# Weighing values for four steps in a row instead of two, with a fifth buffer of exponentials

## The chip, the cores and the metric

The kernel runs on one core of a Trainium2 chip. The metric is the device time of one execution in microseconds (us), lower is better. Its engines: TensorE (PE, matrix products into the eight banks of PSUM), VectorE (DVE), ScalarE (ACT), GpSimd (POOL), and SyncE, which here only issues transfers. Each runs its own list of instructions in order; they meet at semaphores.

## What is computed

One transformer block on x of shape 4 x 2048 x 256: a modulated layer norm, causal attention with 16 heads of 16 columns and rotary position codes, a gated residual; then a second modulated layer norm and a soft mixture of eight experts, with another gated residual. The part that matters here:

```
q, k = rope(h @ Wq.T), rope(h @ Wk.T); v = h @ Wv.T     # 16 heads of 16
scores = einsum('bhqd,bhkd->bhqk', q, k) * scale
scores = where(causal, scores, lowest)
attn = softmax(scores, axis=-1)
out = einsum('bhqk,bhkd->bhqd', attn, v)
```

## The kernel before

The four batches run one after another. In each, attention is followed by the second norm and the experts, beside which the next batch's queries and keys are made. The change touches attention alone.

**Tiling.** Heads are taken four at a time (four groups), and for each group the 2048 queries in four chunks of 512. That makes 16 chunks, k = 0 to 15, with k = 4 * group + c. A **step** is one block of 128 keys against the chunk's 512 queries, for the four heads of the group. Chunk c has 4c full steps and then four on the causal diagonal, which use 512, 384, 256 and 128 queries. That is 4, 8, 12 or 16 steps for a chunk and 160 for a batch. A step is cut into **units**, each of which fills one PSUM bank: a full step has four (one for each head), the diagonal ones four, four, two and one. A batch has 560 units. Three banks (0 to 2) are for scores, used in turn.

**Three streams in PE's list.** (1) Score units: `score_unit` (line 717, with the causal mask added by line 721). It waits until ScalarE has taken the bank's last content. (2) Max units: the running maximum of each query has to be known before its scores are made, so a second set of score products (lines 631 to 642, 592 units a batch) goes to three other banks (3 to 5), and VectorE reduces each to maxima (line 1347, 640 reductions a batch). A max unit waits until VectorE has reduced the bank's last content. Max units run some chunks ahead of the score units; the table `MAXES_BY` fixes how many stand before each score unit, on the whole a little more than one for each. In the last chunk there are none. (3) Weighing: `weigh(s)` (line 737) multiplies the exponentials of step s with the values of its 128 keys, four float32 products, one for each head, side by side in four strips of 32 columns of the array, all added up in bank 6.

**ScalarE** takes each score unit out of PSUM through an exponential (line 1047) into a buffer of exponentials in SBUF: `Eb`, four buffers, step s in buffer s % 4 (`ESLOTS = 4`). At the first unit of a step it waits until the step that had the buffer before is weighed. At the end of a chunk it copies bank 6 out (line 1041).

**VectorE**, beside the reductions, runs at the end of each chunk of maxima a chain of five small operations (lines 1364 to 1373) and a copy (line 1343), and once a chunk it divides the output by the sum (lines 1434 and 1436).

**The order** is written out by hand. After each score unit u, PE runs what `WEIGH_AFTER` has for u: steps are weighed in pairs. Steps s and s + 1 (s even) come three units (`WEIGH_BEHIND`) after the last unit of s + 1. Since every chunk's number of steps is a multiple of four, pairs never cross chunks. In the last chunk, the projection and the second norm of the earlier chunks run beside the scores (`beside`), and the squares of that norm go to the 8 KB behind the other buffers (`squares`, at 14336 of R2).

Of the kernel before, what the change touches and what calls it, by code (L numbers as in the profile page):

```python
# [9 lines left out]
P = 128  # L10
NT = T // P
NC = 4
CH = T // NC
# [12 lines left out]
NST = 3  # L26
# [7 lines left out]
HG = 4  # L34
NG = H // HG
NK = NG * NC
VC = HD + 1


def steps_of_chunk(k):  # L40

    return 4 * (k % NC) + 4


STEPS = [(k, j) for k in range(NK) for j in range(steps_of_chunk(k))]
NSTEP = len(STEPS)
# [4 lines left out]
def diagonal(s):  # L51

    k, j = STEPS[s]
    return max(j - 4 * (k % NC), -1)
# [8 lines left out]
SU = len(UNITS)  # L63
FIRST_UNIT = [[u[0] for u in UNITS].index(s) for s in range(NSTEP)]
LAST_UNIT = [FIRST_UNIT[s + 1] - 1 if s + 1 < NSTEP else SU - 1 for s in range(NSTEP)]
# [75 lines left out]
WEIGH_BEHIND, EVAC_BEHIND, TURN_BEHIND, GATHER_BEHIND = 3, 5, 8, 9  # L141


def after_units(last, behind):

    out = {}
    for i, u in enumerate(last):
        out.setdefault(u + behind, []).append(i)
    return out
# [1 line left out]

LAST_UNIT_OF_CHUNK = [LAST_UNIT[LAST_STEP[k]] for k in range(NK)]

WEIGH_AFTER = after_units([LAST_UNIT[s | 1] for s in range(NSTEP)], WEIGH_BEHIND)
EVAC_AFTER = after_units(LAST_UNIT_OF_CHUNK, EVAC_BEHIND)
TURN_AFTER = after_units(LAST_UNIT_OF_CHUNK, TURN_BEHIND)
GATHER_AFTER = after_units(LAST_UNIT_OF_CHUNK, GATHER_BEHIND)

SLOTS_AFTER = after_units(LAST_UNIT_OF_CHUNK[NC:2 * NC], GATHER_BEHIND + 3)
ESLOTS = 4  # L160

QU = 2 * NC
HIDDEN_BANK = [6, 0]
# [20 lines left out]
def set_of(b, i):  # L184
    return i % SETS_OF_BATCH[b]


def set_parked(b, i):

    before = [(d, j) for d in range(b + 1) for j in range(QU) if d < b or j <= i]  # L190
    return 32 * sum(set_of(d, j) == set_of(b, i) for d, j in before)
# [3 lines left out]
def adaln_block(nc, x, Wq, Wk, Wv, Wo, norm_gamma, slot_gamma, slot_embeds, w1, b1, w2, b2, cond, wmod,  # L195
# [12 lines left out]
    with ctx:  # L208
        def sb(name, shape, dt=f32):
            return ctx.enter_context(nc.sbuf_tensor(name, shape, dt))  # L210

        def sem(name):
            return ctx.enter_context(nc.semaphore(name))
# [41 lines left out]
        R2 = sb("R2", [P, 16384])  # L255
# [3 lines left out]
        def view(r, a, n, dt=f32):  # L259
            v = r[:, a:a + n]  # L260
            return v if dt == f32 else v.bitcast(dt)
# [1 line left out]

        kst = [view(R1, 8192 * i, 4096, bf16).rearrange("p (h t) -> p h t", h=HG) for i in range(2)]
        qst = [view(R1, 8192 * i + 4096, 4096, bf16).rearrange("p (h t) -> p h t", h=HG) for i in range(2)]
        Eb = [view(R2, 2048 * i, 2048).rearrange("p (h t) -> p h t", h=HG) for i in range(ESLOTS)]
        vall = view(R2, 8192, NT * H * VC).rearrange("p (t h c) -> p t h c", t=NT, h=H)
        outT = [view(R2, 12800 + 512 * i, 512) for i in range(2)]
        otok = view(R4, 0, 4096).rearrange("p (t d) -> p t d", d=D)
# [49 lines left out]
        ps = ctx.enter_context(nc.psum_tensor("ps", [P, 8, 512], f32))  # L319
# [40 lines left out]
        s_pk = [sem(f"parts_parked{i}") for i in range(RSETS)]  # L360
# [11 lines left out]
        s_pvq = sem("step_weighted")  # L372
# [183 lines left out]
        def _(pe):  # L556
            mm, tr = nc.tensor.matmul, nc.tensor.transpose
# [3 lines left out]
            for w in range(2):  # L561
                for k in range(KD):
                    for r in range(2):
                        last = tr(ps[:, w, (2 * k + r) * P:(2 * k + r + 1) * P], pw[:, w, r, k * P:(k + 1) * P], ident[:, :])
            last.then_inc(s_pt, 1)
            pe.wait_ge(s_silu, 1)
            for k in range(KD):
                last = tr(ps[:, 4, k * B:k * B + B], pc[0:B, k * P:(k + 1) * P], ident[0:B, 0:B])
# [3 lines left out]
            for i, q in enumerate((0, 1, 6, 7, 2, 3, 8, 9)):  # L572
                for f in range(KD):
                    last = mm(ps[:, 4, P + i * B:P + i * B + B], wmod_sb[:, f, q * P:(q + 1) * P], siluT[:, f, :],
                              start=f == 0, stop=f == 1)
# [115 lines left out]
            for n, bank in ((0, 6), (1, 0)):  # L691
                for f in range(KD):
                    last = mm(ps[0:B, bank, :], siluT[:, f, :], wmod_sb[:, f, (n + 1) * 512:(n + 2) * 512],
                              start=f == 0, stop=f == 1)
# [9 lines left out]
            for b in range(B):  # L704

                def score_unit(u):

                    s, h0, n, w = UNITS[u]
                    k, j = STEPS[s]
                    g, c = divmod(k, NC)  # L710
                    if s == FIRST_STEP[k] and u == FIRST_UNIT[s]:
                        pe.wait_ge(s_bias[k % 3], (b * BIAS_USES[k % 3] + k // 3 + 1) * 64)
                    if u >= NST:
                        pe.wait_ge(s_ex, b * SU + (u + 1 - NST))
                    bank = ps[:, u % NST, :]
                    for i in range(n):
                        last = mm(bank[:, i * w:(i + 1) * w], kst[g % 2][0:BROWS, h0 + i, j * P:(j + 1) * P],  # L717
                                  qst[g % 2][0:BROWS, h0 + i, (c + 1) * CH - w:(c + 1) * CH],
                                  start=i == 0, stop=True, skip_group_check=True)
                    if diagonal(s) >= 0:  # L720
                        last = mm(bank[:, 0:n * w].rearrange("p (n w) -> p n w", n=n)[:, :, 0:P], identb[:, :],  # L721
                                  maskTb[:, 0:n, :], start=False, stop=True, skip_group_check=True)
                    last.then_inc(s_st, 1)

                def weigh(s):

                    k, j = STEPS[s]
                    g, c = divmod(k, NC)
                    w = CH - max(diagonal(s), 0) * P
                    if j == 0:  # L730
                        if k:
                            pe.wait_ge(s_ev, b * NK + k)
                        else:
                            pe.wait_ge(s_vone, b + 1)
                    pe.wait_ge(s_ex, b * SU + (LAST_UNIT[s] + 1))
                    for h in range(HG):
                        last = mm(ps[32 * h:32 * h + VC, 6, CH - w:CH], vall[:, j, HG * g + h, :], Eb[s % ESLOTS][:, h, 0:w],  # L737
                                  start=j == 0, stop=True, skip_group_check=True)
                    last.then_inc(s_pvq, 1)

# [73 lines left out]
                for u in range(SU):  # L814
# [3 lines left out]
                    score_unit(u)  # L818
                    for s in WEIGH_AFTER.get(u, ()):
                        weigh(s)  # L820
# [5 lines left out]
                    if u in BESIDE_AT:  # L826
                        beside(BESIDE_AT.index(u))
                for s in range(NSTEP):
                    if LAST_UNIT[s | 1] + WEIGH_BEHIND >= SU:
                        weigh(s)  # L830

                def logits(n):
# [64 lines left out]
                for n in range(NT):  # L897
# [3 lines left out]
                    for i in range(4):  # L901

                        k, mh = (i % 2, i // 2) if n == NT - 1 else (i // 2, i % 2)
                        last = mm(ps[:, 2 * k + mh, :], xn[:, n, k * P:(k + 1) * P], L[:, n, mh * 512:(mh + 1) * 512],  # L904
                                  start=n == 0, stop=n == NT - 1)
# [63 lines left out]
        def _(act):  # L969
            A = nc.scalar.activation  # L970
# [8 lines left out]
            for w in range(2):  # L979
                for k in range(KD):  # L980
                    last = nc.scalar.copy(wqkT[:, k, 2 * w:2 * w + 2, :].rearrange("p r t -> p (r t)"),
                                          ps[:, w, k * 256:(k + 1) * 256])
# [43 lines left out]
            for e in range(E):  # L1026
                last = A(psquares[:, e, :], pse[:, e, :], ACT.Square, accum_out=ssq[:, e:e + 1])
            last.then_inc(s_pss, 1)

            for b in range(B):  # L1030
# [10 lines left out]
                    nc.scalar.copy(outT[k % 2], ps[:, 6, :]).then_inc(s_ev, 1)  # L1041

                for u, (s, h0, n, w) in enumerate(UNITS):
                    if u == FIRST_UNIT[s] and s >= ESLOTS:
                        act.wait_ge(s_pvq, b * NSTEP + (s + 1 - ESLOTS))
                    act.wait_ge(s_st, b * SU + (u + 1))
                    A(Eb[s % ESLOTS][:, h0:h0 + n, 0:w], ps[:, u % NST, 0:n * w].rearrange("p (n w) -> p n w", n=n),  # L1047
                      ACT.Exp, scale=SCALE).then_inc(s_ex, 1)
                    if u == LAST_UNIT_OF_CHUNK[1]:
                        act.wait_ge(s_out, b * 16 * NC) if b else None  # L1050
                        for i in range(QU - SETS_OF_BATCH[b], QU):
                            act.wait_ge(s_pk[set_of(b, i)], set_parked(b, i))
                        act.wait_ge(s_mpark, 16)
                        load_group(act, 1, slice(0, T), s_ld[1])
                    for g in range(2, NG):
                        if u == LAST_UNIT_OF_CHUNK[NC * (g - 1) - 1]:
                            load_group(act, g, slice(0, T), s_ld[g % 2])
                    for k in EVAC_AFTER.get(u, ()):
                        evacuate(k)
                    if b == 0:  # L1060
                        for j in SLOTS_AFTER.get(u - 2, ()):
                            act.wait_ge(s_pt, 4 + j)
                            k, half = divmod(j, 2)
                            A(snT[:, k, half * 512:(half + 1) * 512], ps[:, 7, :], ACT.Identity, scale=gamcol[:, k:k + 1]
                              ).then_inc(s_pe_, 1)
# [75 lines left out]
                for e in range(E):  # L1141
# [3 lines left out]
                    for j in range(JH):  # L1145
                        last = A(hTe[e % 2][:, j, :], ps[:, HIDDEN_BANK[e % 2] + j // 4, (j % 4) * P:(j % 4 + 1) * P], ACT.Gelu,  # L1146
                                 bias=b1T[:, e * JH + j:e * JH + j + 1])
# [528 lines left out]
```

## Time and profile before

| | us |
|---|---|
| median of 3 runs | 3226.12 |
| lowest and highest | 3223.44, 3234.1 |
| the profiled execution | 3226.97 |
| its span in the trace | 3225.1 |

| engine | busy us | share of the span |
|---|---|---|
| PE | 3028.2 | 94% |
| VectorE | 2249.3 | 70% |
| ScalarE | 1754.8 | 54% |
| GpSimd | 340.8 | 11% |

The page gives busy time over the whole span, which mixes stages with different limits. A busy PE is not one that works at its rate: each matmul is shown with its whole way through the array, about 0.38 us for one of 512 columns, though the next one starts 0.22 us behind it. So what limits a stage is read from the distances between starts, and from the idle time in brackets at the end of a row of the timeline, with the engine and the line that ended it. A row of the timeline merges like instructions that follow each other ("x8"). In rows of line 737, "x16" is a pair of steps: eight products, each recorded as two.

### The profile page before, as it was taken

Reading aid. Unit: us, or ns where it says so; the run is one execution under the profiler, and the core shown is the slowest. Engines: PE = TensorE matmul, PEld = TensorE weight load, DVE = VectorE, ACT = ScalarE, POOL = GpSimd, SP = SyncE. Lnnn points to the kernel's source line nnn. Section 1 sums busy time; section 2 is a strip of 40 time slices with the busy share of each in tenths; the row PEclk is TensorE's granted clock in tenths of the full one; section 3 lists DMA queues with packets and bytes.
Section 4 is the critical chain, followed back from the end, with each engine's and each line's share of the span. In section 5 each row is a group of like instructions: output and inputs, shape, how many; then the busy total and the mean of one; then the engine's idle time right before and its main releaser. Section 6 shows DMA issues by size and latency. Waiting matters only on the chain.

```text
span 3225.1 us, 45179 instructions
## 1 busy us (share of the span) xinstructions
PE 3028.2 (94%) x17474; PEld 1535.5 (48%) x17651; DVE 2249.3 (70%) x4388; ACT 1754.8 (54%) x3189; POOL 340.8 (11%) x196
## 2 busy tenths in 40 slices
PE   6699999989999999998999999999999999999899
PEld 4233334447653333454774333345477333334468
DVE  5888887572778878756388888866448888885722
ACT  3356666564236666645515666664541666665550
POOL 4100000320400000112040000011222000002200
PEclk9899999999999999999999999999999999999999
DMA  5222201015412220002542202000453221100052
GB/s 153 79 41 41 41 1 40 15 57 205 150 35 34 41 41 27 21 7 92 196 138 54 41 1 41 28 21 7 145 178 116 41 41 26 17 27 27 33 180 75
DMA packets 124260, 206.12 MB, mean 64 GB/s; under 512 B 10223, under 2 KB 107189, under 8 KB 120425
## 3 DMA queue, kind: packets, MB, share of 16 engines
q1 hardware_dynamic: 110460, 153.07, 14.5%
q10 hardware_dynamic: 13584, 50.15, 8.4%
q8 instruction: 140, 2.29, 0.3%
q14 instruction: 76, 0.61, 0.1%
HBM read 160.21 MB, written 42.19 MB: 63 GB/s over the span
## 4 chain that ended last, share of the span: by engine, by line
PE 76%; DVE 15%; ACT 5%; issue 2%; ACTq 1%; DMA 1%; POOL 0%; SPq 0%; DVEq 0%
PE ps L737 14%; DVE pm L1347 12%; PE ps L717 9%; PE ps L642 9%; PE ps L904 7%; PE ps L843 7%; PE ps L655 7%; PE ps L935 4%; PE ps L602 3%; PE ps L924 3%; ACT R L1047 2%; PE ps L783 2%; PE ps L676 2%; PE ps L634 2%; PE ps L856 2%
## 5 line engine op out<-in xcount | busy, mean ns | idle before, releaser
L1347 DVE TENSOR_REDUCE pm<-ps 128x1 f32<-128x512 f32 (+4 forms) x2560 | 1380.5, 603 | 292.1 <-PE ps L642 193.5
L1047 ACT ACTIVATE R<-ps 128x512 f32<-128x512 f32 (+1 forms) x2240 | 1177.3, 592 | 652.0 <-PE ps L717 425.0
L717 PE MATMUL ps<-R 99*128 99x512 bf16 (+3 forms) x2560 | 829.8, 350 | 17.6 <-ACT R L1047 7.8
L642 PE MATMUL ps<-R 96*128 96x512 bf16 x1536 | 580.9, 386 | 39.4 <-DVE pm L1347 34.6
L737 PE MATMUL ps<-R 128*17 128x512 f32 (+3 forms) x5120 | 531.6, 533 | 4.9
L642 PEld LDWEIGHTS ps<-R 96*128 96x128 bf16 x1536 | 147.7, 97 | 437.3 <-DVE pm L1347 363.0
L717 PEld LDWEIGHTS ps<-R 99*128 99x128 bf16 x2560 | 241.9, 98 | 155.1 <-ACT R L1047 67.1
L655 PE MATMUL ps<-R 128*128 128x257 f32 x1024 | 247.2, 382 | 7.2 <-ACT R L991 3.6
L737 PEld LDWEIGHTS ps<-R 128*17 128x17 f32 x5120 | 118.2, 97 | 281.9 <-issue 168.4
L904 PE MATMUL ps<-R 128*128 128x512 f32 x512 | 230.0, 611 | 18.0 <-ACT R L1119 18.0
L843 PE MATMUL ps<-snT,R 128*128 128x512 f32 x512 | 230.1, 593 | 0.0
L1221 POOL TENSOR_TENSOR rstd<-veps,neghalf 128x4 f32<-128x4 f32 x16 | 16.2, 1013 | 1859.2 <-DVE veps L1457 1858.8
L655 PEld LDWEIGHTS ps<-R 128*128 128x128 f32 x1024 | 188.9, 190 | 48.4 <-issue 12.8
L904 PEld LDWEIGHTS ps<-R 128*128 128x128 f32 x512 | 99.7, 196 | 150.4 <-issue 140.8
L721 PE MATMUL ps<-maskTb,identb 128*128 128x128 bf16 (+2 forms) x671 | 159.8, 238 | 0.0
L1073 ACT ACTIVATE R<-ps,rnorm 128x1024 f32<-128x1024 f32 x64 | 71.4, 1116 | 147.9 <-PE ps L843 147.9
L1594 DVE TENSOR_TENSOR R<-ps,R 128x256 f32<-128x256 f32 x32 | 13.6, 425 | 187.7 <-PE ps L935 187.7
L843 PEld LDWEIGHTS ps<-snT,R 128*128 128x128 f32 x512 | 92.9, 190 | 94.8 <-issue 94.6
L935 PE MATMUL ps<-R 128*128 128x256 f32 x512 | 123.0, 396 | 9.2 <-ACT R L1146 7.7
L634 PE MATMUL ps<-R 96*128 96x128 bf16 x1024 | 100.6, 220 | 32.2 <-DVE maskTb L1397 13.5
L924 PE MATMUL ps<-R 128*128 128x128 f32 x1024 | 119.3, 275 | 8.5 <-DVE R L1585 8.5
L924 PEld LDWEIGHTS ps<-R 128*128 128x128 f32 x1024 | 118.4, 192 | 13.0 <-DVE R L1585 11.8
(159 smaller groups left out, 3142.8 us busy)
## 6 DMA issues: line engine op xcount, KB each, us to landing
R<-in_L_ffn_w_dram SPq DMA_DIRECT2D x64, 1024.0 KB, 6.1
R<-q_parts ACTq DMA_DIRECT2D x12, 768.0 KB
R<-k_parts ACTq DMA_DIRECT2D x12, 768.0 KB
q_parts<-R SPq DMA_DIRECT2D x16, 512.0 KB, 3.6
k_parts<-R SPq DMA_DIRECT2D x16, 512.0 KB, 3.5
R<-in_L_attn_x_dram SPq DMA_DIRECT2D x4, 2048.0 KB, 8.7
x_park<-R SPq DMA_DIRECT2D x16, 512.0 KB, 2.6
R<-x_park SPq DMA_DIRECT2D x16, 512.0 KB, 5.5
```

What stands on the lines that cost most here:

```text
L634: last = mm(ps[:, bank, i * P:(i + 1) * P], qt(4 * c + i), kt(4 * c + i, 1), start=False, stop=True, skip_group_check=True)
L642: last = mm(ps[:, bank, :], qt(4 * c + r), kt(4 * kc, 4), start=True, stop=True)
L655: last = mm(ps[:, 6 + n % 2, 0:D + 1], EcT[:, e, n * P:(n + 1) * P], eo[:, e, :], start=e == 0, stop=e == E - 1)
L717: last = mm(bank[:, i * w:(i + 1) * w], kst[g % 2][0:BROWS, h0 + i, j * P:(j + 1) * P], qst[g % 2][0:BROWS, h0 + i, (c + 1) * CH - w:(c + ...
L721: last = mm(bank[:, 0:n * w].rearrange("p (n w) -> p n w", n=n)[:, :, 0:P], identb[:, :], maskTb[:, 0:n, :], start=False, stop=True, skip_ ...
L737: last = mm(ps[32 * h:32 * h + VC, 6, CH - w:CH], vall[:, j, HG * g + h, :], Eb[s % ESLOTS][:, h, 0:w], start=j == 0, stop=True, skip_grou ...
L843: last = mm(ps[:, 4 - 2 * (n % 2) + mh, :], xnT[:, k, n * P:(n + 1) * P], snT[:, k, mh * 512:(mh + 1) * 512], start=k == 0, stop=k == 1)
L904: last = mm(ps[:, 2 * k + mh, :], xn[:, n, k * P:(k + 1) * P], L[:, n, mh * 512:(mh + 1) * 512], start=n == 0, stop=n == NT - 1)
L924: last = mm(ps[:, HIDDEN_BANK[e % 2] + j // 4, (j % 4) * P:(j % 4 + 1) * P], w1s[e % NR][:, k, j * P:(j + 1) * P], slotsT[:, k, e * P:(e + ...
L935: last = mm(ps[:, 4 + e % 2, 0:D], hTe[e % 2][:, j, :], w2s[e % NR][:, j, :], start=j == 0, stop=j == JH - 1)
L1047: A(Eb[s % ESLOTS][:, h0:h0 + n, 0:w], ps[:, u % NST, 0:n * w].rearrange("p (n w) -> p n w", n=n), ACT.Exp, scale=SCALE).then_inc(s_ex, 1)
L1347: mx = lambda o, i: V.tensor_reduce(o, i, AX.X, ALU.max)
```

## The change

Weighing is put in groups of four: `weighed_with(s)` gives the step behind whose last unit s is weighed. It is the last of its four steps (s | 3) everywhere but for the full steps of the last chunk, which stay in pairs (s | 1). PE therefore weighs 43 times a batch and not 80.

Four steps stay in their buffers longer, so there are five, the fifth over the place of `squares`. `place_exponentials` gives each step its buffer, its place in it and the step whose weighing frees it. The last diagonal step (128 queries) shares the buffer of the second one, behind its 384 columns. In the last chunk only the first four buffers are handed out. ScalarE waits for the weighing of the step that had the buffer, and at the first use of the fifth in the first batch for a transfer out of the same place.

```diff
+def weighed_with(s):
+
+    return s | 3 if diagonal(s) >= 0 or STEPS[s][0] < NK - 1 else s | 1
+
+
+WEIGH_AFTER = after_units([LAST_UNIT[weighed_with(s)] for s in range(NSTEP)], WEIGH_BEHIND)
-WEIGH_AFTER = after_units([LAST_UNIT[s | 1] for s in range(NSTEP)], WEIGH_BEHIND)
...
-ESLOTS = 4
+
+ESLOTS = 5
+
+
+def place_exponentials():
+
+
+    places, last = [], {}
+    for s in range(NSTEP):
+        if diagonal(s) == 3:
+            places.append((places[s - 2][0], CH - P, None))
+            last[places[s][0]] = s
+            continue
+        slot = min(range(ESLOTS - (STEPS[s][0] == NK - 1)), key=lambda x: last.get(x, x - ESLOTS))
+        places.append((slot, 0, last.get(slot)))
+        last[slot] = s
+    return places
...
-        Eb = [view(R2, 2048 * i, 2048).rearrange("p (h t) -> p h t", h=HG) for i in range(ESLOTS)]
+        Eb = [view(R2, 2048 * i if i < 4 else 14336, 2048).rearrange("p (h t) -> p h t", h=HG) for i in range(ESLOTS)]
...
-                        last = mm(ps[32 * h:32 * h + VC, 6, CH - w:CH], vall[:, j, HG * g + h, :], Eb[s % ESLOTS][:, h, 0:w],
+                        last = mm(ps[32 * h:32 * h + VC, 6, CH - w:CH], vall[:, j, HG * g + h, :], Eb[slot][:, h, at:at + w],
...
-                    if u == FIRST_UNIT[s] and s >= ESLOTS:
-                        act.wait_ge(s_pvq, b * NSTEP + (s + 1 - ESLOTS))
+                    slot, at, freed_by = EPLACES[s]
+                    if u == FIRST_UNIT[s] and freed_by is not None:
+                        act.wait_ge(s_pvq, b * NSTEP + (freed_by + 1))
+                    elif u == FIRST_UNIT[s] and slot == 4 and b == 0:
+
+                        act.wait_ge(s_pk[3], set_parked(0, 3))
```

What this moves in PE's list, at four full steps of chunk 2 in the first batch. Before, with line 737 the weighing (x8 is a pair), 717 a score unit, 642 and 631 to 640 max units; the two pairs stand eight score units apart, and of the rows between them the last ones are shown:

```order
367 L737 MATMUL ps<-R 17x512 x8
368 L642 MATMUL ps<-R 128x512
369 L717 MATMUL ps<-R 128x512
370 L642 MATMUL ps<-R 128x512
...
383 L717 MATMUL ps<-R 128x512
384 L642 MATMUL ps<-R 128x512
385 L717 MATMUL ps<-R 128x512
386 L737 MATMUL ps<-R 17x512 x8
```

Now (line 763 is the weighing, 742 a score unit, 656 to 667 max units), all four stand where the second pair stood:

```order
360 L665 MATMUL ps<-R 128x256
361 L667 MATMUL ps<-R 128x512
362 L742 MATMUL ps<-R 128x512
363 L763 MATMUL ps<-R 17x512 x16
364 L667 MATMUL ps<-R 128x512
365 L742 MATMUL ps<-R 128x512
```

Nothing else has moved against the score units: the max units stand where they did.

On the diagonal, after chunk 2 in the same batch, the first pair stood right behind the chunk's last score unit, and the second three units later:

```order
470 L717 MATMUL ps<-R 128x128 x4
471 L721 MATMUL ps<-maskTb,identb 128x512
472 L737 MATMUL ps<-R 17x512 x4
473 L737 MATMUL ps<-R 17x384 x4
474 L642 MATMUL ps<-R 128x512
475 L717 MATMUL ps<-R 128x512
```

Now the four are together, behind the third unit of the next chunk:

```order
474 L742 MATMUL ps<-R 128x512
475 L746 MATMUL ps<-maskTb,identb 128x128
476 L763 MATMUL ps<-R 17x512 x4
477 L763 MATMUL ps<-R 17x384 x4
478 L763 MATMUL ps<-R 17x256 x4
479 L763 MATMUL ps<-R 17x128 x4
480 L662 MATMUL ps<-R 128x128
```

The products are the same in number and size.

## Rows read from the trace of the kernel before

**Rows 1.** Busy us of PE, PEld, DVE, ACT, POOL, and PE's clock, in a stretch.
```profile
940.00:1312.00 372.00, 357.15 (x2500) 137.40 (x2540) 306.85 (x640) 247.04 (x472) 0.00 (x0) 1.00 0.18 33
```

**Rows 2.** Timeline of PE, steady part: start, length, instructions, [idle before <- what ended it].
```profile
1099.76 0.38 PE L717 MATMUL ps<-R 99*128 99x512 bf16 x1
1100.07 1.91 PE L737 MATMUL ps<-R 128*17 128x512 f32 x16
1101.91 0.39 PE L642 MATMUL ps<-R 96*128 96x512 bf16 x1
1102.14 0.38 PE L717 MATMUL ps<-R 99*128 99x512 bf16 x1
```

**Rows 3.** Timeline of PE's weight loads inside the pair of rows 2.
```profile
1100.51 0.12 PEld L737 LDWEIGHTS ps<-R 128*17 128x17 f32 x4 [0.31 <-issue]
1100.94 0.12 PEld L737 LDWEIGHTS ps<-R 128*17 128x17 f32 x4 [0.31 <-issue]
```

**Rows 4.** Timeline of PE, between two pairs where eight max units meet eight score units.
```profile
1315.46 0.39 PE L642 MATMUL ps<-R 96*128 96x512 bf16 x1
...
1316.06 0.39 PE L642 MATMUL ps<-R 96*128 96x512 bf16 x1
...
1317.79 1.91 PE L737 MATMUL ps<-R 128*17 128x512 f32 x16
```

**Rows 5.** Timeline of VectorE behind the pair of rows 4.
```profile
1320.06 4.74 DVE L1347 TENSOR_REDUCE pm<-ps 128x1 f32<-128x512 f32 x9 [1.07 <-PE ps L642]
```

**Rows 6.** Timeline of VectorE, full steps of chunks 5 to 7, second batch.
```profile
1067.22 6.69 DVE L1347 TENSOR_REDUCE pm<-ps 128x1 f32<-128x512 f32 x12
1075.14 4.88 DVE L1347 TENSOR_REDUCE pm<-ps 128x1 f32<-128x512 f32 x8 [1.23 <-PE ps L642]
...
1089.82 4.88 DVE L1347 TENSOR_REDUCE pm<-ps 128x1 f32<-128x512 f32 x8 [0.45 <-PE ps L642]
1096.00 5.27 DVE L1347 TENSOR_REDUCE pm<-ps 128x1 f32<-128x128 f32 x10 [1.30 <-PE ps L638]
1102.34 3.08 DVE L1347 TENSOR_REDUCE pm<-ps 128x1 f32<-128x512 f32 x5 [1.07 <-PE ps L642]
...
1123.67 5.11 DVE L1347 TENSOR_REDUCE pm<-ps 128x1 f32<-128x256 f32 x10 [0.80 <-PE ps L640]
1130.05 4.67 DVE L1347 TENSOR_REDUCE pm<-ps 128x1 f32<-128x512 f32 x9 [1.27 <-PE ps L642]
1136.07 1.29 DVE L1347 TENSOR_REDUCE pm<-ps 128x1 f32<-128x512 f32 x2 [1.34 <-PE ps L642]
...
1142.94 5.27 DVE L1347 TENSOR_REDUCE pm<-ps 128x1 f32<-128x512 f32 x10 [1.60 <-PE ps L642]
1149.38 4.88 DVE L1347 TENSOR_REDUCE pm<-ps 128x1 f32<-128x512 f32 x8 [1.17 <-PE ps L642]
1155.61 5.27 DVE L1347 TENSOR_REDUCE pm<-ps 128x4 f32<-128x512 f32 x10 [1.36 <-PE ps L634]
```

**Rows 7.** Timeline of VectorE, diagonals of chunks 4, 5 and 6.
```profile
1059.46 1.29 DVE L1347 TENSOR_REDUCE pm<-ps 128x1 f32<-128x512 f32 x2 [0.98 <-PE ps L642]
...
1081.10 1.89 DVE L1347 TENSOR_REDUCE pm<-ps 128x1 f32<-128x512 f32 x3 [1.08 <-PE ps L642]
1083.29 3.67 DVE L1347 TENSOR_REDUCE pm<-ps 128x1 f32<-128x512 f32 x7 [0.30 <-PE ps L642]
...
1114.60 1.09 DVE L1347 TENSOR_REDUCE pm<-ps 128x1 f32<-128x128 f32 x3 [1.70 <-PE ps L638]
1115.72 0.19 DVE L1364 TENSOR_REDUCE negm<-pm 128x16 f32<-128x32 f32 x1
```

**Rows 8.** Timeline of ScalarE beside rows 4.
```profile
1314.34 4.16 ACT L1047 ACTIVATE R<-ps 128x512 f32<-128x512 f32 x8 [1.73 <-PE ps L717]
```

**Rows 9.** Timeline of PE, the pairs on the diagonal of chunk 6.
```profile
1112.54 1.70 PE L737 MATMUL ps<-R 128*17 128x512 f32 x16
...
1115.96 0.84 PE L737 MATMUL ps<-R 128*17 128x256 f32 x16
```

## What the change does to the time: the prediction

> **What bounds the kernel now.** I first read the busy time of a stretch, to see whether one engine fills the stage that the change touches; then the timeline of PE, for the distances between starts; then VectorE's, for when it is idle and what ends that.
>
> In 372 us of the second batch's attention VectorE is busy 306.85 us, ScalarE 247.04 [rows 1]. PE's 357.15 is inflated, since each matmul is shown with its way through the array. From starts: a score or max unit of 512 columns costs PE 0.22 us, and a pair of weighed steps 1.84 us (1100.07 to 1101.91) [rows 2]. Four full steps are 16 score units, about 17 max units and two pairs: 33 x 0.22 + 2 x (1.84 + 0.09) = 11.1 us, the 0.09 being the lag in front of a pair (1099.76 to 1100.07 is 0.31, not 0.22) [rows 2]. They take longer: two pairs lie between the idle times at 1136.07 and 1149.38, 13.31 us apart, and between 1089.82 and 1102.34, 12.52 us [rows 6]. So PE is not at its limit. Rows 4 show why: in that stretch max units start 0.60 us apart (1315.46, 1316.06), not 0.44, and 0.61 is what a VectorE reduction takes (4.88 us for 8) [rows 4, 6]. The three max banks are full, PE waits for VectorE, and since PE's list is in order the scores behind wait too.
>
> VectorE is idle nearly only when PE weighs: it empties its three banks and then waits for the first max unit behind the pair. The idle times in rows 5 to 7 are these. **So the time of this stage is VectorE's work plus its idle time behind the pairs.** The work is untouched. Everything turns on whether the idle time grows or shrinks.
>
> **The switches.** A pair's weight loads come 0.43 us apart [rows 3], so its products need 4 x 0.43 = 1.72 us; it costs 0.09 + 1.84, so 0.21 us is entering and leaving. 37 pairs less in each of four batches, 148, save PE 148 x 0.21 = 31 us. Where PE waits 0.16 us at each max unit (0.60 against 0.44), this only lengthens the wait and is worth nothing. The Trainium skill, TensorEngine Tiling (Array Packing), Key Properties, says that changing the tiling mode drains TensorE; the 0.12 us that a pair takes over its 1.72 are such a price. By that rule alone the time would fall, by the 31 us worked out before.
>
> **Full steps, the main term.** A merged group puts 1.72 us more of weighing into one place. What VectorE can do meanwhile does not grow: it has at most three full banks. At one pair it was saturated: the pair at 1317.79 left it idle for 1.07 us, until 1320.06 [rows 4, 5]. From the pair's end (1317.79 + 1.84 = 1319.63) to VectorE's start are 0.43 us. So 1.84 + 0.43 - 1.07 = 1.20 us is the work it had in store when the pair began. Two saturated pairs leave 2 x 1.07 = 2.14 us idle, one group of four 1.07 + 1.72 = 2.79. The store is used once instead of twice.
>
> Not every pair is saturated, so I take one group of heads, chunks 4 to 7, which has six sets of four full steps. Idle behind the first pair of each, which goes: 0 (the 6.69 us of reductions from 1067.22 run through, since a division and the gate's product were in VectorE's list there), 0.45, 1.07, 0.80, 1.34, 1.17 [rows 6]: 4.83 us. Added behind the second pairs: 6 x 1.72 = 10.32. But five of the second pairs now show 1.23, 1.30, 1.27, 1.60 and 1.36 [rows 6], more than the saturated 1.07, as PE came to them with less in VectorE's banks; with sixteen score units since the last weighing instead of eight the banks will be full, which gives back 6.76 - 5 x 1.07 = 1.41. Net 10.32 - 4.83 - 1.41 = 4.08 us for six, 0.68 each. There are 21 sets a batch; at the last of them the max units end, which leaves 20 x 4 = 80: **+54 us**. Without the giving back a set costs 0.915, +73. If all first pairs were like the saturated one (1.07), with no other work in their shadow, it would be 1.72 - 1.07 - 1.41 / 6 = 0.42, +33.
>
> **Diagonals.** The first pair lasts 1.63 us, the second 0.77 (the rows' 1.70 and 0.84, less the 0.07 by which rows 2's 1.91 exceeds 1.84) [rows 2, 9]; together 2.40. Saturated, they would leave 2.40 + 0.43 - 1.20 = 1.63 idle, against 1.08 + 0.30 at chunk 5 [rows 7]: +0.25, and I take chunk 7 to be like it. At chunk 6 the chain of five small operations starts at 1115.72, just before the second pair, and behind it are the full banks, so VectorE has some 2.0 us in hand by my estimate (0.8 of chain, 1.2 of store); idle becomes 0.83 against 1.70: -0.87 [rows 7, 9]. Chunk 4, like 6 but with 0.98 before [rows 7], gives -0.15. Sum -0.52 for four; 56 diagonals with max units around them are 14 fours: **-7 us**. It lies between +14 (all like chunk 5) and -20.
>
> **The rest.** ScalarE needs 0.52 us for a unit (4.16 for 8) and waits 1.73 us behind a pair [rows 8]. With four steps it waits some 3.5, and 16 x 0.52 = 8.3 us fit into the 9.6 that remain of 13.1. Its waits for buffers: a set's second step takes the buffer of the first step of the set before; that one is weighed first in a group which stands before the second step's scores in PE's list, so the wait ends first. The fifth buffer's wait in the first batch is for a transfer made before attention begins: nothing. The last set of chunk 14 and its diagonal come when the maxima are done; two switches less are -2 us for four batches, a delay of 1.84 us for each batch would be +7; I take 0, as neither engine is full there. The last chunk keeps its pairs, and its diagonal steps come at the end in either order.
>
> **Sum.** 54 - 7 = +47 us. On the profiled execution (3226.97 us, of which 3225.1 are its span) that is 3274; it stands 0.85 us over the median, so 3273 for a median.
>
> **Rivals.** (1) *PE is the bound after all.* If VectorE's store were larger than I read, the longer weighing would be covered, PE's waits for it would go, and the 31 us of switches would come back: 3195. For it: PE's high busy time in rows 1, and in rows 2 a pair that starts right behind its score unit. Against: the 0.60 us steps of rows 4. A set now has 4.83 + 6.76 us over six of them, 1.9 us, of idle; to stay under that, a group of four would need 0.9 us more in store than the 1.20 seen. (2) *Balance.* A set costs the 0.42 of the lower bound, diagonals give back 20 and the end 2: 33 - 20 - 2 = +11, or somewhat less: 3227 to 3237. For it: unsaturated pairs such as the 1.60. (3) *More.* No giving back, diagonals at +14, the end at +7: +94, 3320. For it: first pairs with 0 and 0.45, whose weighing was nearly free.
>
> The Trainium skill, TensorEngine Tiling (Array Packing), PSUM Bottleneck, warns that packing speeds up TensorE but not the emptying of PSUM; the trace agrees, since max units wait for reductions of 0.61 us each. It changes nothing in the sum and speaks for the forecast against rival 1.
>
> **How the numbers follow.** The store of three banks explains all idle times of VectorE read here, so the forecast with its spread (3237 to 3320) has 0.74; balance 0.12, PE as the bound 0.13, beyond 3320 0.01. A measurement of this kernel can tell about 0.3% (10 us) from no change, so balance is nearly all of "same". Faster 0.13, same 0.12, slower 0.75. The range 3226 to 3310 leaves out the faster case and the highest end.
>
> **What would show it.** In the profile after: a group of four lasting 3.56 us; VectorE idle 2.6 to 2.9 us behind most of them at full steps, and 0.8 to 1.6 on diagonals; max units 0.60 us apart over most of a set, not only at its end; a set of four full steps 0.7 us longer; no idle of ScalarE that a weighing ended. I am wrong if the idle behind a group stays near 1.9 us, or if VectorE's reductions themselves become shorter.

## The result: 2.1% slower

| | median us | lowest to highest | runs |
|---|---|---|---|
| before | 3227.57 | 3223.44 to 3234.1 | 4 |
| changed | 3296.41 | 3292.98 to 3298.38 | 4 |

The ratio is 1.021, with a 95% interval of 1.019 to 1.0231: 69 us more. Forecast were 47 more (3273 for the median, 3226 to 3310 the range). The span of the profiled execution went from 3225.1 to 3291.1 us.

Two rows of the page carry the reading. They are the reductions of the maxima and the exponentials, with busy time, mean length, and the idle time of their engine just before them:

```profile
L1377 DVE TENSOR_REDUCE pm<-ps 128x1 f32<-128x512 f32 (+4 forms) x2560 | 1370.8, 600 | 362.8 <-PE ps L667 201.7
L1077 ACT ACTIVATE R<-ps 128x512 f32<-128x512 f32 (+1 forms) x2240 | 1189.9, 594 | 706.0 <-PE ps L742 395.3
```

Before, the page had these two as:

```profile
L1347 DVE TENSOR_REDUCE pm<-ps 128x1 f32<-128x512 f32 (+4 forms) x2560 | 1380.5, 603 | 292.1 <-PE ps L642 193.5
L1047 ACT ACTIVATE R<-ps 128x512 f32<-128x512 f32 (+1 forms) x2240 | 1177.3, 592 | 652.0 <-PE ps L717 425.0
```

VectorE does the same 2560 reductions, and is idle 70.7 us longer in front of them; its busy time is 9.7 us less. The sum of both has grown by 61 of the 66 us. So the time is where the prediction looked for it. (Why busy time shrinks: reductions that follow each other overlap a little. The rows show 0.67 to 0.69 us for one alone and 4.88 for eight, 0.61 each. Fewer interruptions, more overlap.)

One thing beside it differs. TensorE's granted clock has two levels, 2.4 and 1.2 GHz, and its mean, as a share of the full clock, is 0.980 in this profile and 0.986 in the one before: about 130 us at the lower level against 90. Much of the difference lies in the first chunks of the first batch (from 130 to 195 us the mean is 0.84, before 0.97). What this is worth is taken up with the sum below.

The timeline of PE, at the second set of chunk 7 in the second batch. A group of four stands there, and behind it max units (line 667) and score units (line 742) in turn:

```profile
1171.06 0.38 PE L742 MATMUL ps<-R 99*128 99x512 bf16 x1
1171.36 3.63 PE L763 MATMUL ps<-R 128*17 128x512 f32 x32
1174.92 0.39 PE L667 MATMUL ps<-R 96*128 96x512 bf16 x1
...
1176.10 0.39 PE L667 MATMUL ps<-R 96*128 96x512 bf16 x1
1176.33 0.38 PE L742 MATMUL ps<-R 99*128 99x512 bf16 x1
1176.70 0.39 PE L667 MATMUL ps<-R 96*128 96x512 bf16 x1
1176.92 0.38 PE L742 MATMUL ps<-R 99*128 99x512 bf16 x1
1177.29 0.39 PE L667 MATMUL ps<-R 96*128 96x512 bf16 x1
```

From 1171.36 to 1174.92 are 3.56 us, twice 1.72 and 0.12: one switch is saved. From 1176.10 on the max units start 0.60 and 0.59 us apart, as in rows 4: PE waits for VectorE again. VectorE's timeline around it:

```profile
1162.18 5.87 DVE L1377 TENSOR_REDUCE pm<-ps 128x1 f32<-128x512 f32 x11 [2.99 <-PE ps L667]
...
1171.23 0.21 DVE L1373 COPY nrow<-ps 48x128 bf16<-48x128 bf16 x1
1171.36 0.67 DVE L1377 TENSOR_REDUCE pm<-ps 128x1 f32<-128x512 f32 x1
1175.35 10.05 DVE L1377 TENSOR_REDUCE pm<-ps 128x1 f32<-128x512 f32 x18 [3.31 <-PE ps L667]
1188.47 1.68 DVE L1377 TENSOR_REDUCE pm<-ps 128x4 f32<-128x512 f32 x4 [3.07 <-PE ps L659]
```

Idle 2.99, 3.31 and 3.07, and between them no pause of VectorE of 0.15 us or more. At the same three places rows 6 have 1.27, 1.60 and 1.36. Each has grown by 1.71 or 1.72 us, the two steps' weighing that was put there. The first pairs' 0.80, 1.34 and 1.17 are gone. The other three sets of rows 6, in chunks 5 and 6, do the same:

```profile
1104.75 6.67 DVE L1377 TENSOR_REDUCE pm<-ps 128x1 f32<-128x512 f32 x11 [2.94 <-PE ps L667]
...
1126.81 8.26 DVE L1377 TENSOR_REDUCE pm<-ps 128x1 f32<-128x128 f32 x15 [3.02 <-PE ps L663]
...
1139.92 0.69 DVE L1377 TENSOR_REDUCE pm<-ps 128x4 f32<-128x512 f32 x1 [2.15 <-PE ps L659]
```

The first two were 1.23 and 1.30, and the third was 0.43, in a row of before that rows 6 leave out:

```profile
1108.56 0.69 DVE L1347 TENSOR_REDUCE pm<-ps 128x4 f32<-128x512 f32 x1 [0.43 <-PE ps L634]
```

The diagonals of chunks 5 and 6:

```profile
1112.92 3.67 DVE L1377 TENSOR_REDUCE pm<-ps 128x1 f32<-128x512 f32 x7 [1.51 <-PE ps L667]
...
1148.96 1.13 DVE L1377 TENSOR_REDUCE pm<-ps 128x1 f32<-128x256 f32 x2 [0.85 <-PE ps L665]
```

Forecast were 1.63 and 0.83, from 1.38 and 1.70 [rows 7]. The other two that the forecast used came out otherwise: at chunk 4 it is 0.32 where 0.83 was worked out, and at chunk 7 the diagonal's idle time went from 2.91 to 2.31, where +0.25 was taken.

To compare kernels, I add up VectorE's idle times in the timeline (those shown, from about 0.15 us up) between the start of a set's first weighing and the start of the next set's, over the 80 sets of full steps and the 56 diagonals with max units around them:

| | idle per set of full steps | idle per diagonal | sum against before | span against before |
|---|---|---|---|---|
| before | 2.03 | 1.53 | | |
| changed | 3.05 | 1.35 | +82 - 10 = +72 | +66.0 |

### The profile page after: what moved, and what is told of

It reads as the page before. It is cut to its first block, busy times and chain, and to the rows that moved or that the text cites. A ratio compares the mean times of both kernels' runs of the same rounds, so it can differ in the third digit from the quotient of the medians.

```text
span 3291.1 us, 45128 instructions
## 1 busy us (share of the span) xinstructions
PE 3067.5 (93%) x17489; PEld 1540.4 (47%) x17651; DVE 2250.1 (68%) x4388; ACT 1766.9 (54%) x3189; POOL 340.2 (10%) x196
## 3 DMA queue, kind: packets, MB, share of 16 engines
q1 hardware_dynamic: 110460, 153.07, 14.3%
## 4 chain that ended last, share of the span: by engine, by line
PE 73%; DVE 18%; ACT 5%; issue 2%; DMA 1%; SPq 1%; ACTq 0%; POOL 0%; DVEq 0%
PE ps L763 15%; DVE pm L1377 15%; PE ps L667 8%; PE ps L742 8%; PE ps L930 7%; PE ps L869 7%; PE ps L680 7%; PE ps L961 4%; PE ps L627 3%; PE ps L950 3%; ACT R L1077 2%; PE ps L809 2%; PE ps L701 2%; PE ps L882 1%; PE ps L659 1%
## 5 line engine op out<-in xcount | busy, mean ns | idle before, releaser
L1377 DVE TENSOR_REDUCE pm<-ps 128x1 f32<-128x512 f32 (+4 forms) x2560 | 1370.8, 600 | 362.8 <-PE ps L667 201.7
L1077 ACT ACTIVATE R<-ps 128x512 f32<-128x512 f32 (+1 forms) x2240 | 1189.9, 594 | 706.0 <-PE ps L742 395.3
L667 PE MATMUL ps<-R 96*128 96x512 bf16 x1536 | 588.4, 391 | 69.0 <-DVE pm L1377 59.9
L763 PE MATMUL ps<-R 128*17 128x512 f32 (+3 forms) x5120 | 506.6, 535 | 0.6
L763 PEld LDWEIGHTS ps<-R 128*17 128x17 f32 x5120 | 133.3, 98 | 313.4 <-issue 249.8
```

The lines of the kernel that those rows point to most:

```text
L667: last = mm(ps[:, bank, :], qt(4 * c + r), kt(4 * kc, 4), start=True, stop=True)
L1077: A(Eb[slot][:, h0:h0 + n, at:at + w], ps[:, u % NST, 0:n * w].rearrange("p (n w) -> p n w", n=n), ACT.Exp, scale=SCALE).then_inc(s_ex, 1)
L1377: mx = lambda o, i: V.tensor_reduce(o, i, AX.X, ALU.max)
```

## The experiments

All are variants of the changed kernel, so their line numbers are those of the profile after. Ratios are against runs of the kernel before on the same chip.

| run | median us | ratio | 95% interval |
|---|---|---|---|
| e1_pairs_five_buffers | 3224.36 | 0.9996 | 0.9986 to 1.0006 |
| e2_four_at_full_steps | 3290.41 | 1.0200 | 1.0185 to 1.0215 |
| e3_four_at_diagonals | 3221.85 | 0.9986 | 0.9976 to 0.9995 |
| e4_one_at_a_time | 3245.43 | 1.0060 | 1.0045 to 1.0075 |
| e5_short_maxima_pairs | 3122.28 | 0.9682 | 0.9669 to 0.9695 |
| e6_short_maxima_fours | 3125.20 | 0.9691 | 0.9678 to 0.9704 |
| e7_short_maxima_ones | 3200.03 | 0.9920 | 0.9906 to 0.9933 |
| e8_ones_in_last_chunk | 3217.36 | 0.9973 | 0.9964 to 0.9983 |
| e9_maxima_between_fours | 3257.34 | 1.0094 | 1.0080 to 1.0107 |
| e10_fours_at_diagonals_ones_last | 3211.52 | 0.9955 | 0.9942 to 0.9967 |
| e11_changed_again | 3295.66 | 1.0207 | 1.0190 to 1.0223 |
| e12_four_at_full_again | 3289.49 | 1.0198 | 1.0182 to 1.0214 |

### The buffers alone

```diff
 def weighed_with(s):
-    return s | 3 if diagonal(s) >= 0 or STEPS[s][0] < NK - 1 else s | 1
+    return s | 1
```

> The changed kernel, but every step is weighed with its pair as before; the five buffers, their places and their waits stay. Theory (the loss is VectorE's idle time behind longer weighings): 3227 us, nothing within 10 us of the kernel before. Rival (the loss comes from the fifth buffer: its place, or ScalarE's new waits): 3296 us or most of the way to it.

It is the kernel before within 0.1%. With pairs, the fifth buffer, its place and its waits cost nothing, and all of the loss comes from weighing in fours.

### Fours at full steps, and at diagonals

```diff
-    return s | 3 if diagonal(s) >= 0 or STEPS[s][0] < NK - 1 else s | 1
+    return s | 3 if diagonal(s) < 0 and STEPS[s][0] < NK - 1 else s | 1
```

> Four in a row at full steps only, the diagonal steps in pairs as before. Theory: the traces put +82 us on the 80 sets of full steps and -10 us on the diagonals, so without the diagonals' merging this is slower than the changed kernel: about 3306 us (3300 to 3315). Rival (long weighings cost the same wherever they stand, 148 merges sharing 69 us): 84 of 148 merges, 3227 + 39 = 3266 us.

```diff
-    return s | 3 if diagonal(s) >= 0 or STEPS[s][0] < NK - 1 else s | 1
+    return s | 3 if diagonal(s) >= 0 else s | 1
```

> Four in a row at diagonal steps only, full steps in pairs. Theory: VectorE's idle time falls by about 10 us there, 3217 us (3210 to 3225). Rival (every merge costs alike): 64 of 148 merges, 3227 + 30 = 3257 us.

The full steps alone give the whole loss; 64 of the 148 merges, those on the diagonals, are no loss and between pairs a gain of 4 us. A price for each merge, the same wherever it stands, falls: it asked for 3266 and 3257. My own number for the full steps was wrong too, by 16 us: I had added VectorE's 82 us of idle time without what is given back elsewhere. In the trace of e2 the idle time per set is 3.00 and per diagonal 1.58, +80 us, and the span grew by 66.8. The page's row for the reductions:

```profile
L1377 DVE TENSOR_REDUCE pm<-ps 128x1 f32<-128x512 f32 (+4 forms) x2560 | 1370.8, 601 | 366.9 <-PE ps L667 230.1
```

Busy and idle together are 65.1 us more than before, 74.8 of idle time less 9.7 given back by overlap of the reductions. That is nearly the whole 66.8.

The table's sets leave out the end of chunk 14 and the last chunk. There the merged diagonals do something that the forecast had at nothing. From the first score unit of the last chunk to its last, PE's timeline has 43.4 us in every batch before, in e1 and in e2, and 44.9 in every batch of e3 and of the changed kernel: 6 us for four batches. ScalarE's row behind that weighing, in the second batch, before and after:

```profile
1346.98 1.08 ACT L1047 ACTIVATE R<-ps 128x512 f32<-128x512 f32 x2 [2.32 <-PE ps L717]
```

```profile
1383.11 1.08 ACT L1077 ACTIVATE R<-ps 128x512 f32<-128x512 f32 x2 [3.82 <-PE ps L742]
```

The four diagonal steps of chunk 14 now stand together, three units into the last chunk, and ScalarE waits for the scores behind them: 1.50 us more. Against this stands the end of chunk 14. From the first score unit of its full set to the last chunk there are 25.2 us before, 23.4 in e3, 26.9 in e2 and 25.1 in the changed kernel.

> The changed kernel once more, beside e12 on the same chip. The theory has merged diagonals as a small gain in it: this should be 4 to 10 us under e12_four_at_full_again. The first two measurements had it 6 us over (3296 against 3290), on different chips.

> Fours at full steps, pairs at the diagonals, as e2_four_at_full_steps. Theory: 4 to 10 us over e11_changed_again. If it is equal or under it, what the merged diagonals give back between pairs is lost again between fours.

They came out at 3295.66 (3286.55 to 3299.72) and 3289.49 (3286.14 to 3298.11). The runs overlap, so nothing can be said on which is faster; that merged diagonals gain 4 us or more beside merged full steps, as I expected, is not confirmed. Idle per diagonal is 1.34 against 1.58 in the two traces, -13 us, but per full set it is 3.09 against 2.90, +15. Set by set, these 15 have two sources. Nine sets during which the granted clock fell to 1.2 GHz in one trace or the other, eight of them in e11, hold 8.9 us. The other 6.1 are a matter of counting: they lie in the set just before the diagonal of a chunk with eight full steps, and since the merged diagonal is weighed later, that set's stretch ends later and takes in idle time that e12 has in the diagonal's. All other sets agree within 0.05 us. So the diagonals give back about 7 us here and not 13, and the last chunk takes 6 of them.

### One step at a time

```diff
-    return s | 3 if diagonal(s) >= 0 or STEPS[s][0] < NK - 1 else s | 1
+    return s if STEPS[s][0] < NK - 1 else s | 1
```

> The other way: each step weighed by itself, three units behind its last unit, but for the last chunk, which keeps pairs. Theory: a full step's weighing is 0.86 + 0.12 us and 0.43 to the first maximum, against 1.20 us in VectorE's banks, so 0.2 us idle behind each; a set of four then takes PE's own time, 33 x 0.22 + 4 x 1.07 = 11.5 us instead of 12.6: 80 x -1.0 = -80 us, with something more from the diagonals: 3110 to 3170 us. Rival (entering and leaving the weighing is what costs, 0.21 us each): 72 more in each of four batches, +60 us, 3287 us.

A miss: 3245, slower than before by 20 us, where I expected 80 us less. The rival's +60 is as far off. PE's timeline around a single step, and VectorE's:

```profile
1137.54 0.38 PE L742 MATMUL ps<-R 99*128 99x512 bf16 x1
1137.85 1.05 PE L763 MATMUL ps<-R 128*17 128x512 f32 x8
1138.83 0.39 PE L667 MATMUL ps<-R 96*128 96x512 bf16 x1
```

```profile
1139.26 2.94 DVE L1377 TENSOR_REDUCE pm<-ps 128x1 f32<-128x512 f32 x6 [0.51 <-PE ps L667]
1142.62 2.48 DVE L1377 TENSOR_REDUCE pm<-ps 128x1 f32<-128x512 f32 x4 [0.42 <-PE ps L667]
```

The step costs what I said (0.98 us), but VectorE is idle 0.4 to 0.6 us behind it and not 0.2: 1.82 a set, hardly less than the 2.03 of pairs. Its store is not full when PE comes, because PE, with two switches more in a set, is no longer the one that waits: in front of this step max units start 0.44 us apart, PE's own pace, and not 0.60.

```profile
1136.88 0.38 PE L667 MATMUL ps<-R 96*128 96x512 bf16 x1
1137.10 0.38 PE L742 MATMUL ps<-R 99*128 99x512 bf16 x1
1137.32 0.38 PE L667 MATMUL ps<-R 96*128 96x512 bf16 x1
```

And the row of the reductions says what broken sequences cost:

```profile
L1377 DVE TENSOR_REDUCE pm<-ps 128x1 f32<-128x512 f32 (+4 forms) x2560 | 1401.9, 603 | 285.0 <-PE ps L667 200.1
```

Idle time is 7.1 us less than before, but busy time 21.4 more, so together 14.3 of the 19.6 us by which the span grew. My expectation had priced PE's own time from starts of plain units (11.5 us a set) and left out masks, the turned outputs and the rows.

### Short maxima: VectorE far from its limit

The same edit, in all three groupings (pairs, fours, single steps):

```diff
-                    last = mx(of[:, r, 2 + kc:3 + kc], ps[:, bank, :])
+                    last = mx(of[:, r, 2 + kc:3 + kc], ps[:, bank, 0:P])
```

> Pairs everywhere, with the five buffers. VectorE reduces only 128 of the 512 columns of each full max block (line 1377's branch for whole blocks), so maxima over the other 384 are left out and outputs are not the reference's; everything PE, ScalarE and the semaphores do stays. Theory: with VectorE far from its limit a set takes PE's own 11.1 to 11.4 us instead of 12.6: 3060 to 3130 us. Rival (PE is the bound as it is): 3227 us, no change.

> The changed kernel with the same short maxima as e5_short_maxima_pairs (the same part of the maxima left out). Theory: merging cost time only through VectorE, so here it saves its switches against the short pairs: 148 x 0.21 = -31 us at best, -10 us if ScalarE, whose three banks empty in 1.6 us of the 3.6 us weighing, takes VectorE's place. Rival (long weighings cost by themselves): +60 to +70 us against the short pairs, as without short maxima.

> One step at a time but in the last chunk, with the same short maxima (the same part left out). It measures what entering and leaving the weighing costs where PE is the bound: 72 more in each of four batches, 288 x 0.21 = +60 us against the short pairs. If it were +10 or less, the one-at-a-time kernel must have lost its time to something else than switches.

With less work for VectorE and nothing else changed, pairs take 3122 us, 102 less. So PE is not the bound of the kernel as it is, and rival 1 of the prediction falls. On this ground fours cost 3 us and not 69: **the loss of the change needs a VectorE that is the limit.** But the 31 us of switches do not come either, nor the 10 us less that I expected with ScalarE in VectorE's place: the last chunks take 6.0 us more, as with long maxima, and all the rest only some 3 to 4 less. ScalarE's timeline says why; fours, then pairs:

```profile
1107.75 8.18 ACT L1077 ACTIVATE R<-ps 128x512 f32<-128x512 f32 x16 [3.45 <-PE ps L742]
```

```profile
1099.04 4.26 ACT L1077 ACTIVATE R<-ps 128x512 f32<-128x512 f32 x8 [1.73 <-PE ps L742]
1104.82 4.03 ACT L1077 ACTIVATE R<-ps 128x512 f32<-128x512 f32 x8 [1.51 <-PE ps L742]
```

With fours, ScalarE works without a pause through the set's sixteen units and then waits 3.45 us for the next group: 8.18 + 3.45 = 11.6 us. It has become the limit, just as VectorE was. With pairs a set is 8.29 + 3.24 = 11.5 us. Single steps are 78 us slower than pairs here (3200 against 3122), where 60 were expected, for 288 switches more: 0.27 us each if all of it is switches, near the 0.21 read from the rows. So a switch has a real price, and it is paid where PE is the bound, which is so with single steps; from pairs to fours another engine is in the way, with long maxima and with short ones.

### Max units between the steps of a group

```diff
+                    lead = max(0, 3 - since // 4)
-                    while m < MAXES_BY[b][u]:
+                    while m < min(MAXES_BY[b][u] + lead, MAXES_BY[b][min(u + 4, SU - 1)]):
                         max_unit(b, m)
                         m += 1
                     score_unit(u)
+                    since += 1
-                    for s in WEIGH_AFTER.get(u, ()):
+                    for i, s in enumerate(WEIGH_AFTER.get(u, ())):
+                        if i == 2:
+                            since = 0
+                            for _ in range(3):
+                                if m < MAXES_BY[b][min(u + 4, SU - 1)]:
+                                    max_unit(b, m)
+                                    m += 1
                         weigh(s)
```

> The changed kernel, weighing in fours where it does, but between the second and the third step of a group PE makes the next three max units, which refill VectorE's banks; of the following units some come without a max unit, until PE's list is where it was. Scores, buffers and the time at which steps are weighed stay as in the changed kernel. Theory (what costs is the stretch without max units): idle per set goes from 3.05 us back to 1.9 to 2.5, so 3220 to 3260 us. Rival (late weighing, or the fours with their buffers and ScalarE's longer waits): about 3296 us, or more by the new switches.

3257 us, 39 under the changed kernel. PE and VectorE, at the place shown before (second set of chunk 7):

```profile
1155.48 1.91 PE L763 MATMUL ps<-R 128*17 128x512 f32 x16
1157.33 0.82 PE L667 MATMUL ps<-R 96*128 96x512 bf16 x3
1158.08 1.91 PE L763 MATMUL ps<-R 128*17 128x512 f32 x16
1159.92 0.39 PE L667 MATMUL ps<-R 96*128 96x512 bf16 x1
```

```profile
1157.75 1.89 DVE L1386 TENSOR_REDUCE pm<-ps 128x1 f32<-128x512 f32 x3 [1.60 <-PE ps L667]
1160.34 8.26 DVE L1386 TENSOR_REDUCE pm<-ps 128x1 f32<-128x512 f32 x15 [0.71 <-PE ps L667]
```

Four steps are weighed within 4.4 us, as late as in the changed kernel and with its buffers, but VectorE is idle 1.60 + 0.71 = 2.31 us and not 3.31. Per set of full steps it is 2.14, against 3.05 and against 2.03 before. So it is neither the late weighing nor the four together, but the unbroken stretch without a max unit. It is still 30 us slower than before. On the full steps only 9 us are left; on the diagonals the idle time is 1.89, against 1.53 before and 1.35 in the changed kernel, 20 us over before. All the new waits of one line stand there, and my edit made them. Two rows of VectorE's waits (who waited for whom, us in total, times, longest):

```profile
DVE pm L1386 <- PE ps L667: 158.4, 188, 5.4
DVE rden L1473 <- PE ps L775: 85.9, 52, 11.2
```

In the changed kernel the second of these rows reads as follows, and the kernel before has the same three numbers in it:

```profile
DVE rden L1464 <- PE ps L775: 44.9, 4, 11.2
```

With max units drawn forward, VectorE comes to the division of an output sooner than PE has turned the output, 41 us in 48 new waits, all of them on diagonals. In front of the reductions themselves it is idle 272.7 us, less than the 292.1 of the kernel before. Whether the edit with the division moved along would beat pairs was not tried.

### The last chunk, and the two gains together

```diff
-    return s | 3 if diagonal(s) >= 0 or STEPS[s][0] < NK - 1 else s | 1
+    return s if STEPS[s][0] == NK - 1 else s | 1
```

> Pairs everywhere but in the last chunk of each batch, where each step is weighed alone. There are no max units there, and ScalarE takes VectorE's part: three score banks of 0.52 us, idle 1.18 us behind each pair, 5.2 us from pair to pair. Theory: a single step's 0.98 us is covered by ScalarE's banks, so its idle goes from 1.18 to about 2 x 0.25 for eight units, 0.7 x 5 pairs x 4 batches = -14 us: 3212 us (3208 to 3220). Rival (switches): 7 more in each batch, 28 x 0.21 = +6 us: 3232 us.

3217.36 us, a ratio of 0.9973: 7 us less than before, half of what I expected, and of the sign that the stores give. ScalarE in the second batch's last chunk:

```profile
1374.29 2.06 ACT L1077 ACTIVATE R<-ps 128x512 f32<-128x512 f32 x4 [0.32 <-PE ps L742]
1376.68 2.06 ACT L1077 ACTIVATE R<-ps 128x512 f32<-128x512 f32 x4 [0.33 <-PE ps L742]
```

Four units are 2.39 us apart, so eight 4.78, where pairs took 5.20:

```profile
1372.04 4.03 ACT L1047 ACTIVATE R<-ps 128x512 f32<-128x512 f32 x8 [1.18 <-PE ps L717]
1377.24 4.03 ACT L1047 ACTIVATE R<-ps 128x512 f32<-128x512 f32 x8 [1.18 <-PE ps L717]
```

The idle time is near the 0.25 expected, but an unbroken row of eight exponentials took 4.03 us and two rows of four take 4.12, and in the first half of the chunk other work of PE and VectorE sets the pace.

```diff
+    if STEPS[s][0] == NK - 1:
+        return s
-    return s | 3 if diagonal(s) >= 0 or STEPS[s][0] < NK - 1 else s | 1
+    return s | 3 if diagonal(s) >= 0 else s | 1
```

> Pairs at full steps, fours at the diagonals of all chunks but the last, single steps in the last chunk: the two edits that were each slightly faster. If they add up: -4 and -7 us against the kernel before, 3214 us (3209 to 3220). If each was chance: 3225 us.

3211.52 us, ratio 0.9955 (0.9942 to 0.9967). The two add up, and this version beats both kernels: 16 us under the kernel before (0.45%), 85 under the changed one.

## Why the prediction held, and where its terms were off

**What bounds the kernel.** Right, and shown: taking work from VectorE alone saved 102 us (e5).

**The switches.** 0.21 us each, worth nothing where VectorE is the limit. The size was about right (0.27 in e7), and so was the worth. That they are worth nothing even with a faster VectorE, because ScalarE steps in (e6), I had not considered.

**Full steps, +54 forecast, +82 in idle time.** The mechanism is the one found: each kept place shows its old idle time plus 1.72 us. The term that was mis-sized is the giving back. I took idle times over 1.07 us for pairs to which PE came with VectorE's banks not full, and expected them to shrink once it had sixteen units to fill them. They did not shrink at all: the five places with 6.76 us before have 15.33. This much of the third rival's condition ("no giving back") came true. What differs from place to place is not how many banks are full but, as I read the rows, what is in them and what comes next. Before the 1.60, one of the three max units in store is a row turn that VectorE copies in 0.20 us, and the single reduction left takes 0.67; behind the group at 1.36, the next max unit begins with the mask and four small products, so that its result comes later. These are places in the list, and they stay. Without the giving back my own number was 0.915 a set, +73. The six sets that I had read measure 0.98, and so do, on average, the 74 sets in which the clock stayed at 2.4 GHz both before and after (72 us). The six others hold 9.5 us, 1.6 each: the clock fell in them, in one trace or the other.

**Overlap of reductions.** Left out of the sum. It gives 9.7 us back.

**Diagonals, -7 forecast, -10 in idle time.** Right in sign, and near in size partly by luck: chunks 5 and 6 came out as worked out (1.51 and 0.85 us for 1.63 and 0.83), but in the same group chunks 4 and 7 lost 0.67 and 0.60 where -0.15 and +0.25 were taken, and others changed little (chunk 11: 1.80 to 1.79). Alone (e3) merged diagonals gain 4 us. Beside merged full steps the gain could not be measured.

**The rest, 0 forecast.** Nothing for the fifth buffer's place (e1). But the last chunk, where I had named +7 and taken 0, costs 1.5 us in each batch, 6 in all (e3 and the changed kernel). And there are waits for buffers, which I had ruled out. ScalarE's idle times that a weighing ended, after and before:

```profile
ACT R L1077 <- PE ps L763: 34.7, 12, 3.7
```

```profile
ACT R L1047 <- PE ps L737: 26.0, 7, 4.3
```

The trace of e3 has the same twelve and e2 has three, so they come with the merged diagonals; since e3 is faster than before, they cost little or nothing.

**The clock.** Not in the forecast. The nine runs of the changed kernel (here and in e11) have a mean granted clock of 0.979 to 0.982, the 43 runs of the kernel before that stand beside the experiments 0.982 to 0.987, so the lower clock goes with the change. It is not the main cause: the profiled run of e12, which weighs full steps in fours too, has 0.985, and its span is still 59 us over that of before. An estimate of its share: among the 43 runs a clock lower by 0.001 goes with a time longer by 2.1 us, which makes some 9 us for the 0.0044 between the means. Which of the new waits brings the clock down was not tried.

**Sum.** 82 - 10 = 72 by idle time, less the 9.7 of overlap is 62, and 6 in the last chunks make 68, against 66.0 in the span; the clock's share is inside the idle times. The forecast of 47 had the main term too low by 28, and left out two terms that nearly cancel (-9.7 and +6).

**The signs named beforehand.** A group of 3.56 us: so it is. Idle 2.6 to 2.9 us behind most: the right kind but more, mostly 2.8 to 3.3. On diagonals 0.8 to 1.6: so on average (1.35), but single ones from 0.31 to 2.80. Max units 0.60 us apart over most of a set: yes. A set 0.7 us longer: 1.0 of idle time. No idle time of ScalarE that a weighing ended: missed.

## What to carry to other kernels

Where an engine in order feeds two others through a few banks each, long work for its own account is free only as far as the others have banks in store, and each such stretch uses the store once: cut the stretches, rather than join them, down to the length that the store covers, and stop where the cost of entering them makes the feeder the limit. Read that length from the idle time behind a stretch, stretch by stretch, since it depends on what lies in the banks at that place. A saving on an engine that the trace shows waiting is worth nothing, and when the engine it waits for is relieved, see who is next before counting it.

## What the runs showed of the hardware

A reduction or an exponential costs more when it stands alone than in an unbroken row. VectorE's 128x512 reduction takes 0.67 to 0.69 us alone and 0.60 to 0.61 in a row; over 2560 reductions the same work was 1370.8 us busy with fours, 1380.5 with pairs and 1401.9 with single steps. ScalarE's exponential of a bank takes 0.60 us alone and 0.51 in a row of eight or sixteen. Cutting up a long stretch of another engine therefore has a price there too.

TensorE's granted clock can be part of the price of a reordering. The same products in another order had a mean of about 0.981 of the full clock, against 0.985 before (nine and 43 runs), and most of the added time at 1.2 GHz lay in the first batch.
